# Adapter MLP kernel: a B table stored twice with one gather DMA a sequence, plain products in the first step, and the sums of h stored from the sync queue

## The chip, the cores and the metric

One core of one Trainium2 chip. The metric is the device time of one execution in microseconds; lower is better. Engines are named as the profile names them: PE (TensorE), DVE (VectorE), ACT (ScalarE), POOL (GpSimd), SP (SyncE, which here only issues DMAs).

## The reference

64 sequences of 64 tokens, width 512, each with an adapter number 0 to 7 (`itok_B_0_7`, known only when the kernel runs).

```
def lora_linear(x, W, A, B, a):             # A: (8, in, 16), B: (8, 16, out)
    return x @ W + (x @ A[a]) @ B[a]
gate, up = lora_linear(x, Wg, Ag, Bg, a), lora_linear(x, Wu, Au, Bu, a)   # 512 -> 2048
h = silu(gate) * up
x = x + lora_linear(h, Wd, Ad, Bd, a)       # 2048 -> 512
x = x + einsum('bct,bcd->bdt', x, W1[a])    # a 64x64 matrix a sequence
```

## The kernel before

Everything is float32 from split operands: each operand is cut into a rounded part (`hi`, made by ACT, type fp32r) and the rest (`lo`, made by DVE as source minus hi), and a product is three matmuls, hi*hi, hi*lo, lo*hi (`prod`, L1368 to L1370). On top of that lies one level of a Winograd form of Strassen: a 2x2 block product costs 7 products (P1 to P7) of combined blocks instead of 8 plain ones. The combined blocks of x are T1, T2, T3, NT4 (DVE, `x_add`), those of the weights S1 to S4 (DVE, `w_add`); ACT and DVE put the results together with `keep_p1`, `keep_p5`, `keep_u2`, `make_u3`, `make_c11` and so on.

Stage one (about 0 to 822 us) makes h. It goes over 4 groups of 16 sequences (1024 tokens) and, in each, over 16 chunks of 128 columns of gate and up: 64 steps. A step is 7 products of 6 matmuls of 128x512 and 4 `lora` calls of 4 matmuls of 128x256 (L1380). Stage two (from 822 us) does the down projection in 16 pairs of tiles, reading h back from DRAM (`h_dram`).

The adapter's B rows of two chunks (a "piece") for all 16 sequences of the group lie in `bq[n % 2]`, double-buffered. Each sequence takes part in two halves of the partitions (`half`), so SP issues two DMAs of 16 rows of 4 KB a sequence (`gather_b`, L276): 32 a piece, half of them in each of two steps. They can start when the buffer is free (`p4_done`) and PE needs them in the first `lora` of every second step. The table they read, `b_dram`, holds the split B; in group 0 it is made piece by piece (`load_b`, `b_hi` on ACT, `b_lo` and `store_b` on POOL). Piece 0 skips it: `gather_raw` on SP, `bq0_hi` on ACT, `bq0_lo` on POOL. The adapter's A matrices lie in SBUF (`a_all`), and POOL copies them out sequence by sequence (`gather_a`, L447) for `lora_a` (L1398), which makes x @ A for a group.

SP works through one list in program order: for each step s the weights of step s + 2 (`load_w`, L236), the stores of h of step s - 1 (`store_even`, `store_odd`, L245; these wait for DVE's h), eight sequences of the gather, and in the third step of a group the four x blocks of the next group, 2 MB (`load_x`, L241). The sums of h blocks that the Strassen form of stage two needs (HS1 to HS4, `make_s1` to `make_s4` on DVE) are stored by POOL (`store_sum`, L473), which waits for each. DVE waits for such stores before it writes a sum's tile again.

`step_0` is written out by hand on every engine. On PE it holds the 7 products with the `lora_a` calls between them, and it waits for T1 to NT4 and S1 to S4 of the first step.

## Time and profile before

| | us |
|---|---|
| median of 3 runs | 1217.3 (1215.41 to 1223.75) |
| the profiled execution | 1219.65 |
| its span, first to last instruction | 1218.0 |
| PE, DVE, ACT, POOL busy | 1163.6, 913.6, 539.3, 256.3 |
| mean granted TensorE clock | 0.982 |

Busy times are sums over the span. A granted clock of 1.00 is 2.4 GHz and one of 0.50 is 1.2 GHz.

### The profile page before, as it was taken

What the parts mean: (1) busy time and instruction counts of PE and PEld (TensorE: products, weight loads), DVE (VectorE), ACT (ScalarE), POOL (GpSimd) and SP (SyncE); (2) the same over time, 40 slices, a digit from 0 to 9 for tenths busy, and PEclk for the clock granted to TensorE, in tenths of its full rate; (3) what the DMA queues carried; (4) which work ended last, traced back from release to release, by engine and by line L of the source; (5) the groups of instructions that cost most, each with busy time, mean ns of one, the idle gap of its engine ahead of it and who ended that gap; (6) DMA issues with size and microseconds to landing.
All of it is one profiled execution on the core that took longest, in us unless ns stands there. A gap on an engine that the chain in (4) does not pass through costs nothing.

```text
span 1218.0 us, 23035 instructions
## 1 busy us (share of the span) xinstructions
PE 1163.6 (96%) x6720; PEld 1034.8 (85%) x6720; DVE 913.6 (75%) x1578; ACT 539.3 (44%) x902; POOL 256.3 (21%) x405
## 2 busy tenths in 40 slices
PE   4889999999999997999999999998899999999998
PEld 3678888887888886888888788887899999999997
DVE  6776777876787787678887788888667766776775
ACT  4544444543444443344453344456344444444442
POOL 5223221112201012220101111011322221231230
PEclk8899999999999999899999999999999999999999
DMA  5597876688667589666759978868777777667781
GB/s 188 161 308 241 244 222 180 170 235 262 189 180 234 171 238 264 190 194 187 233 166 274 280 223 252 243 215 307 244 265 244 244 239 273 232 230 274 231 277 66
DMA packets 155583, 276.26 MB, mean 227 GB/s; under 512 B 28898, under 2 KB 97634, under 8 KB 155330
## 3 DMA queue, kind: packets, MB, share of 16 engines
q1 hardware_dynamic: 133104, 213.48, 57.5%
q0 software_dynamic: 21488, 59.66, 14.6%
q10 hardware_dynamic: 866, 1.66, 0.4%
q8 instruction: 54, 0.88, 0.3%
q14 instruction: 71, 0.58, 0.2%
HBM read 200.23 MB, written 74.45 MB: 226 GB/s over the span
## 4 chain that ended last, share of the span: by engine, by line
PE 73%; SPq 9%; DVE 5%; DMA 5%; issue 4%; ACT 3%; POOL 1%; POOLq 0%; DVEq 0%; ACTq 0%
PE ps L1368 12%; PE ps L1369 12%; PE ps L1370 12%; PE ps L1517 8%; PE ps L1519 8%; PE ps L1518 8%; PE ps L1380 7%; SPq L276 7%; DMA bq<-b_dram 2%; PE ps L1398 2%; DMA h_raw<-h_dram 1%; DMA xst<-xg 1%; SPq L245 1%; ACT xo_hi L602 1%; SPq L199 1%
## 5 line engine op out<-in xcount | busy, mean ns | idle before, releaser
L1368 PE MATMUL ps<-xo_hi,w_hi 128*128 128x512 f32 x896 | 359.3, 401 | 12.0 <-DVE w_lo L886 10.7
L1369 PE MATMUL ps<-xo_lo,w_hi 128*128 128x512 f32 x896 | 354.8, 396 | 0.0
L1370 PE MATMUL ps<-xo_hi,w_lo 128*128 128x512 f32 x896 | 351.8, 393 | 0.0
L1368 PEld LDWEIGHTS ps<-xo_hi,w_hi 128*128 128x128 f32 x896 | 171.4, 191 | 43.0 <-DVE w_lo L886 10.7
L1370 PEld LDWEIGHTS ps<-xo_hi,w_lo 128*128 128x128 f32 x896 | 170.4, 190 | 38.2
L473 POOL DMA_DIRECT2D h_dram<-hs x128 | 96.0, 754 | 487.3 <-DVE hs L1001 247.9
L886 DVE TENSOR_TENSOR hl<-h_raw,hh 128x1024 fp32r<-128x1024 f32 x112 | 137.0, 1223 | 79.0 <-ACT hh L602 77.6
L1380 PEld LDWEIGHTS ps<-t_st,bq 128*128 128x128 f32 x1024 | 158.5, 193 | 44.2 <-DMA bq<-b_dram 18.0
L1369 PEld LDWEIGHTS ps<-xo_lo,w_hi 128*128 128x128 f32 x896 | 171.1, 191 | 26.6
L1380 PE MATMUL ps<-t_st,bq 128*128 128x256 f32 x1024 | 166.2, 286 | 21.7 <-DMA bq<-b_dram 15.9
L602 ACT ACTIVATE hh<-h_raw 128x1024 fp32r<-128x1024 f32 x112 | 117.9, 1053 | 113.3 <-DMA h_raw<-h_dram 72.0
L886 DVE TENSOR_TENSOR w_lo<-wsum,w_hi 128x512 fp32r<-128x512 f32 x116 | 83.1, 717 | 60.2 <-ACT w_hi L602 60.2
L674 ACT ACTIVATE u_s<-u_s 128x512 f32<-128x512 f32 x64 | 40.5, 633 | 145.6 <-DVE u_s L973 145.6
L1517 PE MATMUL ps<-wd_t,hh 128*128 128x256 f32 x256 | 73.2, 286 | 5.5 <-DVE hl L886 3.8
L1517 PE MATMUL ps<-wd,hh 128*128 128x288 f32 x256 | 76.6, 299 | 0.0
L986 DVE TENSOR_TENSOR h_f<-u_s,v 128x512 f32<-128x512 f32 x64 | 44.2, 690 | 41.7 <-ACT u_s L674 41.7
L1518 PE MATMUL ps<-wd,hh 128*128 128x288 f32 x256 | 75.4, 295 | 0.0
L670 ACT ACTIVATE p_s<-p_s 128x512 f32<-128x512 f32 x64 | 40.5, 633 | 78.5 <-DVE p_s L956 78.4
L1519 PE MATMUL ps<-wd,hl 128*128 128x288 f32 x256 | 75.2, 294 | 0.0
L602 ACT ACTIVATE w_hi<-wsum 128x512 fp32r<-128x512 f32 x116 | 72.2, 623 | 5.4 <-DVE wsum L919 5.4
L1518 PE MATMUL ps<-wd_t,hh 128*128 128x256 f32 x256 | 72.9, 285 | 0.0
L1519 PE MATMUL ps<-wd_t,hl 128*128 128x256 f32 x256 | 72.9, 285 | 0.0
(153 smaller groups left out, 2188.0 us busy)
## 6 DMA issues: line engine op xcount, KB each, us to landing
bq<-b_dram SPq DMA_DIRECT2D x992, 64.0 KB, 2.6
h_raw<-h_dram SPq DMA_DIRECT2D x112, 512.0 KB, 5.3
h_dram<-hs POOLq DMA_DIRECT2D x128, 256.0 KB, 4.2
raw<-packed SPq DMA_DIRECT2D x58, 512.0 KB, 4.0
...
xs<-x POOLq DMA_DIRECT2D x16, 512.0 KB, 5.8
...
```

Source lines behind the costliest of these rows:

```text
L276: sp.dma_start(bq[n % 2][r:r + RANK, b // QS, :, :].bitcast(F32).rearrange("r k c -> r (k c)"), b_dram[piece_of(g, k), bass.ds(slot_number ...
L473: pool.dma_start(h_dram[PPG * g:PPG * (g + 1), op, :, k, :].rearrange("q p t -> p q t"), tile[:, col:col + HALF].rearrange("p (q t) -> p q ...
L602: return act.activation(dst, src, ACT.Copy)
L886: return dve.tensor_tensor(dst, src, hi.bitcast(F32), ALU.subtract)
L986: dve.tensor_tensor(h_f[s % 2][:, HALF:GT], u2_s[:, :], v22[:, :], ALU.mult).then_inc(h2_done, 1)
L1368: pe.matmul(bank, st[0], mv[0], start=start and kk == 0, stop=False, skip_group_check=True)
L1369: pe.matmul(bank, st[0], mv[1], start=False, stop=False, skip_group_check=True)
L1370: m = pe.matmul(bank, st[1], mv[0], start=False, stop=kk == 1, skip_group_check=True)
L1380: m = pe.matmul(bank[:, i * QT:(i + 1) * QT], b[:, q, c % PIECE, a:a + P], t_st[u][g % 2][:, q * QT:(q + 1) * QT], start=start and part == ...
L1517: pe.matmul(bank[:, 0:width], h_hi, w[:, 0:width], start=start and k == 0, stop=False, skip_group_check=True)
L1518: pe.matmul(bank[:, 0:width], h_hi, w[:, width:2 * width], start=False, stop=False, skip_group_check=True)
L1519: return pe.matmul(bank[:, 0:width], h_lo, w[:, 0:width], start=False, stop=False, skip_group_check=True)
```

## The change

- **B table.** `b_dram` gets a dimension of two copies; `store_b` writes each piece twice (two DMAs). A sequence's 32 rows (two halves of 16) are then one block, fetched by one DMA of 32 rows of 4 KB into every fourth partition (`b % QS:P:QS`). 16 gathers a piece instead of 32. For piece 0 the host gives `b_twice`, a doubled input, and `gather_raw` issues 16 DMAs instead of 32. `slot_mask` and the A operand change their order of rows to match.
- **A.** `a_all` and its 512 KB load go. POOL fetches a sequence's A (128 rows of 512 B, 64 KB) by a DMA each, from DRAM, four a quad, 16 a group; ACT (first group) or POOL (`order_a`, one 512-column copy a quad) puts it in order.
- **First step.** PE does 8 plain products (48 matmuls instead of 42) of the blocks B11, B12, B21, B22 and the raw weights, which need no T or S. T1 to NT4 are made later, for step 1; S1 to S4 of step 0 are not made. The results need no `keep_p1`, `keep_p5`, `keep_u2`, `make_u3` in step 0. The first product of step 1 (`first_product`) is put ahead of the last two `lora` calls of step 0. T3 and `bq0_lo` go from POOL to DVE.
- **Stores of the sums.** `store_s12`, `store_s3`, `store_s4` go from POOL to SP, behind the gathers of the same step; the last ones (`n == 8`, `n == 11` of stage two) too. POOL's list in a step is then `order_a`, `gather_a`, tables, and `b_lo`, `store_b`, `load_b`.
- The waits that counted the removed operations are counted anew (`w_added`, `p1_kept`, `u3_done` one less).

In the diff below, left out are the renamed semaphores, the counts of waits, the row orders and the helpers that only cut a known operation into parts (`w_hi_first`, `w_lo_first`: columns 0 to 255, 256 to 767, 768 to 1023 of the weights).

```
-        b_dram = nc.dram_tensor("b_dram", (PIECES, ADAPTERS, RANK, PIECE * BC), F32, kind="Internal").ap()
+        b_dram = nc.dram_tensor("b_dram", (PIECES, ADAPTERS, 2, RANK, PIECE * BC), F32, kind="Internal").ap()
...
             def load_w(s):
                 n = load_no(s)
-                if n >= 2:
+                if n == 2:
+                    sp.wait_ge(w_lo_done, 3)
+                if n >= 3:
                     sp.wait_ge(w_lo_done, 3 * (n - 2) + 1)
-                    sp.wait_ge(w_added, 4 * (n - 1))
+                    sp.wait_ge(w_added, 4 * (n - 2))
                 sp.dma_start(raw[s % 2][:, :], packed[chunk_of(s)]).then_inc(w_in[s % 2], 16)
 
...
+            def store_s3(n):
+                sp.wait_ge(hs3_done, n + 1)
+                store_op(2 * n, HS3, hs3, 0)
+
+            def store_s12(n):
+                sp.wait_ge(hs1_done, n + 1)
+                store_op(2 * n, HS1, hs1, 0)
+                sp.wait_ge(hs2_done, n + 1)
+                store_op(2 * n, HS2, hs2, 0)
+
+            def store_s4(n):
+                sp.wait_ge(hs4_done, n + 1)
+                store_op(2 * n, HS4, hs2, 0)
+
...
                 slot_numbers[b] = number(sp, b)
-                for half in range(2):
-                    r = half * QR + (b % QS) * RANK
-                    sp.dma_start(bq_raw[r:r + RANK, b // QS, :, :],
-                                 b_gu[0, bass.ds(slot_numbers[b], 1)].rearrange("a r k c -> (a r) k c"))\
-                        .then_inc(bq_raw_in[2 * b // SLOTS], 16)
+                sp.dma_start(bq_raw[b % QS:P:QS, b // QS, :, :].rearrange("r k c -> r (k c)"),
+                             b_twice[bass.ds(slot_numbers[b], 1)].rearrange("a r c -> (a r) c"))\
+                    .then_inc(bq_raw_in[2 * b // SLOTS], 16)
 
             def gather_b(n, first, last):
                 g, k = divmod(n, PIECES)
-                sp.wait_ge(b_stored, 16 * (k if g == 0 else PIECES))
+                sp.wait_ge(b_stored, 32 * (k if g == 0 else PIECES))
                 if n >= 2:
                     sp.wait_ge(p4_done, 2 * n - 2)
                 for b in range(first, last):
-                    for half in range(2):
-                        r = half * QR + (b % QS) * RANK
-                        sp.dma_start(bq[n % 2][r:r + RANK, b // QS, :, :].bitcast(F32).rearrange("r k c -> r (k c)"),
-                                     b_dram[piece_of(g, k), bass.ds(slot_numbers[g * SLOTS + b], 1)].rearrange("a r c -> (a r) c"))\
-                            .then_inc(bq_in[n % 4], 16)
+                    sp.dma_start(bq[n % 2][b % QS:P:QS, b // QS, :, :].bitcast(F32).rearrange("r k c -> r (k c)"),
+                                 b_dram[piece_of(g, k), bass.ds(slot_numbers[g * SLOTS + b], 1)].rearrange("a e r c -> (a e r) c"))\
+                        .then_inc(bq_in[n % 4], 16)
...
                     gather_b(s // 2 + 1, at, at + SLOTS // 2)
+                if s % 2:
+                    store_s3(s // 2)
+                    if s >= 3:
+                        store_s4(s // 2 - 1)
+                else:
...
         def _(pool):
             def gather_a(g, q):
                 if g:
-                    pool.wait_ge(t_done, g * QUADS + q)
+                    pool.wait_ge(a_ordered, g * QUADS + q)
                 for s in range(QS):
                     a = number(pool, g * SLOTS + q * QS + s)
-                    pool.tensor_copy(aq[q if g == 0 else 0][:, :, s, :], a_all[:, bass.ds(a, 1), :, :].rearrange("p a k r -> p (a k) r"))\
-                        .then_inc(a_gathered, 1)
+                    pool.dma_start(a_raw[0 if g else q + 1][:, s, :, :].rearrange("p k r -> p (k r)"),
+                                   a_gu[bass.ds(a, 1)].rearrange("a p c -> (a p) c")).then_inc(a_in[q], 16)
+
+            def order_a(g, q):
+                pool.wait_ge(a_in[q], 16 * QS * (g + 1))
+                pool.wait_ge(t_done, g * QUADS + q)
+                pool.tensor_copy(aq[0][:, :, :, :], a_raw[0][:, :, :, :].rearrange("p s k r -> p k r s")).then_inc(a_ordered, 1)
...
             def store_b(i):
                 pool.wait_ge(b_lo_done, i + 1)
-                pool.dma_start(b_dram[(i + 1) % PIECES].rearrange("a r c -> (a r) c"),
-                               b_hl[:, :, :].bitcast(F32).rearrange("p k c -> p (k c)")).then_inc(b_stored, 16)
-
...
 
             load_b(0)
-            pool.wait_ge(x_in[B12], 16)
-            pool.wait_ge(x_in[B22], 16)
-            pool.tensor_tensor(xst[T3][:, :], xst[B22][:, :], xst[B12][:, :], ALU.subtract).then_inc(t3_first, 1)
+            pool.wait_ge(idx_in, 16)
+            for q in range(QUADS):
+                gather_a(0, q)
             b_lo(0)
             store_b(0)
-            pool.wait_ge(idx_in, 16)
-            pool.wait_ge(a_in, 16)
-            for q in range(QUADS):
-                gather_a(0, q)
             load_b(1)
-            for pair in range(2):
-                bq0_lo(pair)
             for s in range(1, STEPS):
                 g, c = divmod(s, CH)
                 late = LATE_T if g == 0 else 0
+                if g + 1 < GROUPS and 4 <= c - late < 8:
+                    order_a(g + 1, c - late - 4)
+                if g + 1 < GROUPS and 3 <= c - late < 7:
+                    gather_a(g + 1, c - late - 3)
+                if s == 2 * CH:
+                    load_tables()
+                if s == 2 * CH + 3:
+                    store_tables()
                 if s < PIECES:
                     b_lo(s)
                     store_b(s)
                     if s + 1 < PIECES:
                         load_b(s + 1)
-                if g + 1 < GROUPS and 4 <= c - late < 8:
-                    gather_a(g + 1, c - late - 4)
-                if s == 2 * CH:
-                    load_tables()
...
             act.dma_start(idx_i[0:1, :], idx).then_inc(idx_in, 16)
             act.dma_start(xst[B21][:, :], xg[0, :, B21]).then_inc(x_in[B21], 16)
             act.dma_start(xst[B22][:, :], xg[0, :, B22]).then_inc(x_in[B22], 16)
-            act.dma_start(a_all[:, :, :, :], a_gu).then_inc(a_in, 16)
             act.dma_start(smask[:, :], slot_mask).then_inc(const_in, 16)
             act.dma_start(tmask[:, :], tok_mask).then_inc(const_in, 16)
...
+            def order_a_first(q):
+                act.wait_ge(a_in[q], 16 * QS)
+                hi(aq[q][:, :, :, :], a_raw[q + 1][:, :, :, :].rearrange("p s k r -> p k r s")).then_inc(a_ordered, 1)
...
+            w_hi_first(0)
+            w_hi_first(1)
             x_first(B21)
+            w_hi_first(2)
+            x_hi_b12()
+            x_first(B22)
+            order_a_first(0)
             b_hi(0)
-            w_hi_sum(0, 0)
-            keep_p1(0)
+            w_hi_raw(1)
+            order_a_first(1)
             x_first(T1)
             x_first(T2)
-            w_hi_sum(0, 1)
+            bq0_hi(0)
+            order_a_first(2)
+            t_hi(0, 0)
+            w_hi_sum(1, 0)
+            t_hi(0, 1)
+            order_a_first(3)
+            t_hi(0, 2)
             x_first(T3)
-            x_first(B22)
-            t_hi(0, 0)
-            keep_p5(0)
-            x_first(NT4)
-            t_hi(0, 1)
-            keep_u2(0)
-            w_hi_raw(1)
-            t_hi(0, 2)
-            bq0_hi(0)
-            w_hi_sum(1, 0)
+            bq0_hi(1)
             t_hi(0, 3)
             w_hi_sum(1, 1)
-            bq0_hi(1)
             silu_1(0)
+            keep_p1(1)
             silu_2(0)
+            x_first(NT4)
             act.wait_ge(const_in, 48)
             hi(eye_r[:, :], eye_f[:, :])
...
+            def keep_c11_first():
+                dve.wait_ge(p2_done, 1)
+                dve.tensor_copy(p1_s[:, :], RB[0]).then_inc(c11_done, 1)
+
+            def keep_c22_first():
+                dve.wait_ge(l22_done, 1)
+                dve.tensor_copy(v22[:, :], RD).then_inc(v22_done, 1)
+
+            def keep_c12_first():
+                dve.wait_ge(p3_done, 1)
+                dve.tensor_copy(u2_s[:, :], RC[0]).then_inc(c12_done, 1)
...
@@ -1177,44 +1212,48 @@
                 x_lo(0, XOPS.index(op))
 
             x_first(B11)
-            w_lo_raw(0)
+            w_lo_first(0)
+            w_lo_first(1)
             x_first(B21)
-            for k in range(4):
-                w_add(0, k)
+            w_lo_first(2)
+            x_lo_b12()
+            x_first(B22)
             x_add(0, 1, None)
-            w_lo_sum(0, 0)
             x_add(0, 2, None)
-            x_first(T1)
-            x_first(T2)
-            w_lo_sum(0, 1)
-            dve.wait_ge(const_in, 48)
-            t_mask(0, 0)
-            x_first(T3)
-            t_lo(0, 0)
-            x_add(0, 3, None)
-            x_first(B22)
-            t_mask(0, 1)
-            x_first(NT4)
-            t_lo(0, 1)
             for k in range(4):
                 w_add(1, k)
             w_lo_raw(1)
+            x_first(T1)
+            x_first(T2)
+            bq0_lo(0)
+            dve.wait_ge(const_in, 48)
+            t_mask(0, 0)
+            t_lo(0, 0)
+            w_lo_sum(1, 0)
+            t_mask(0, 1)
+            x_add(0, 0, None)
+            t_lo(0, 1)
             t_mask(0, 2)
-            make_u3(0)
             t_lo(0, 2)
-            w_lo_sum(1, 0)
+            x_first(T3)
             t_mask(0, 3)
+            bq0_lo(1)
             t_lo(0, 3)
+            keep_c11_first()
             w_lo_sum(1, 1)
-            make_c11(0)
-            make_c22(0)
-            make_c12(0)
+            keep_c22_first()
+            make_h1(0)
+            keep_c12_first()
+            x_add(0, 3, None)
+            make_h2(0)
+            x_first(NT4)
             for s in range(1, STEPS - 1):
                 g, c = divmod(s, CH)
                 first, last = c == 0 and g > 0, c == CH - 1 and g + 1 < GROUPS
...
+            def ready(op):
+                pe.wait_ge(x_lo_done, x_turn(0, XOPS.index(op)) + 1)
+
+            def plain(bank, w, k, start, x_hi_sem, x_lo_sem, x_count, w_count):
+                wc = [slice(w * WB + kk * P, w * WB + (kk + 1) * P) for kk in range(2)]
+                xc = [slice(kk * HALF, (kk + 1) * HALF) for kk in range(2)]
+                pe.wait_ge(w_hi_done, w_count)
+                pe.wait_ge(x_hi_sem, x_count)
+                for kk in range(2):
+                    pe.matmul(bank, w_hi[0][:, wc[kk]], xo_hi[k][:, xc[kk]], start=start and kk == 0, stop=False,
+                              skip_group_check=True)
+                pe.wait_ge(x_lo_sem, x_count)
+                for kk in range(2):
+                    pe.matmul(bank, w_hi[0][:, wc[kk]], xo_lo[k][:, xc[kk]], start=False, stop=False, skip_group_check=True)
+                pe.wait_ge(w_lo_done, w_count)
+                for kk in range(2):
+                    m = pe.matmul(bank, w_lo[0][:, wc[kk]], xo_hi[k][:, xc[kk]], start=False, stop=kk == 1,
+                                  skip_group_check=True)
+                return m
+
             def step_0():
-                def ready(op):
-                    pe.wait_ge(x_lo_done, x_turn(0, XOPS.index(op)) + 1)
-
-                pe.wait_ge(w_lo_done, 1)
-                ready(B11)
-                prod(RA[0], 0, A11, 0, True).then_inc(p1_done, 1)
-                ready(B21)
-                prod(RB[0], 0, A12, 3, True)
+                a11, a12, a22, a21 = range(4)
+                plain(RB[0], a11, 0, True, x_hi_done, x_lo_done, 1, 1).then_inc(p1_done, 1)
+                plain(RB[0], a12, 3, False, x_hi_done, x_lo_done, 2, 2).then_inc(p5_done, 1)
+                plain(RA[0], a22, 3, True, x_hi_done, x_lo_done, 2, 2).then_inc(p6_done, 1)
+                plain(RA[0], a21, 0, False, x_hi_done, x_lo_done, 1, 3)
                 lora_a(0, 0)
+                plain(RC[0], a11, 6, True, b12_hi_done, b12_lo_done, 1, 1)
+                plain(RD, a21, 6, True, b12_hi_done, b12_lo_done, 1, 3).then_inc(p7_done, 1)
                 lora_a(0, 1)
-                pe.wait_ge(w_lo_done, 2)
-                ready(T1)
-                prod(RC[0], 0, S1, 1, True).then_inc(p5_done, 1)
+                plain(RC[0], a12, 5, False, x_hi_done, x_lo_done, 3, 2)
                 lora_a(0, 2)
-                pe.wait_ge(p1_kept, 1)
-                ready(T2)
-                prod(RA[0], 0, S2, 2, False).then_inc(p6_done, 1)
+                plain(RD, a22, 5, False, x_hi_done, x_lo_done, 3, 2)
                 lora_a(0, 3)
-                pe.wait_ge(u2_kept, 1)
-                pe.wait_ge(w_lo_done, 3)
-                ready(T3)
-                prod(RA[0], 0, S3, 4, False).then_inc(p7_done, 1)
-                pe.wait_ge(p5_kept, 1)
-                ready(B22)
-                prod(RC[0], 0, S4, 5, False)
-                pe.wait_ge(u3_done, 1)
-                ready(NT4)
-                prod(RA[0], 0, A22, 6, False)
                 pe.wait_ge(bq0_lo_done, 1)
                 pe.wait_ge(t_lo_done, 4)
                 lora(RB[0], 0, 0, 0, False).then_inc(p2_done, 1)
                 lora(RA[0], 0, 1, 0, False).then_inc(p4_done, 1)
+                first_product(1)
                 pe.wait_ge(bq0_lo_done, 2)
                 pe.wait_ge(t_lo_done, 2 * QUADS)
-                lora(RD, 0, 1, 1, True).then_inc(l22_done, 1)
+                lora(RD, 0, 1, 1, False).then_inc(l22_done, 1)
                 lora(RC[0], 0, 0, 1, False).then_inc(p3_done, 1)
+
+            def first_product(s):
+                g, c = divmod(s, CH)
+                pe.wait_ge(w_lo_done, 3 * load_no(s) + 1)
+                if c == 0:
+                    pe.wait_ge(x_lo_done, 7 * g + 1)
+                if s == 1:
+                    pe.wait_ge(t_masked, 2)
+                if s >= 2:
+                    pe.wait_ge(h1_done, s - 1)
+                prod(RA[s % 2], s, A11, 0, True).then_inc(p1_done, 1)
```

## Rows read from the trace of the kernel before

**Rows 1.** Busy time by stretch: us, PE, PEld, DVE, ACT, POOL busy, clock, DMA share, GB/s.

```profile
225.00:425.00 200.00, 198.00 (x992) 167.70 (x991) 155.22 (x257) 89.68 (x144) 32.29 (x48) 1.00 0.71 208
```

**Rows 2.** Who PE waited for: us in total, times, longest us.

```profile
PE ps L1380 <- DMA bq<-b_dram: 15.9, 5, 7.2
PE ps L1380 <- POOL bq L468: 5.9, 2, 3.7
PE ps L1398 <- POOL aq L447: 4.9, 1, 4.9
```

**Rows 3.** Timeline of PE, first matmuls of steps 0 and 2: start, us.

```profile
10.73 0.79 PE L1368 MATMUL ps<-xo_hi,w_hi 128*128 128x512 f32 x1 [10.73 <-DVE w_lo L886]
60.13 0.40 PE L1368 MATMUL ps<-xo_hi,w_hi 128*128 128x512 f32 x1
60.36 0.40 PE L1369 MATMUL ps<-xo_lo,w_hi 128*128 128x512 f32 x1
```

**Rows 4.** The profile's chain that ended last, by line.

```profile
PE ps L1368 12%; PE ps L1369 12%; PE ps L1370 12%; PE ps L1517 8%; PE ps L1519 8%; PE ps L1518 8%; PE ps L1380 7%; SPq L276 7%; DMA bq<-b_dram 2%; PE ps L1398 2%; DMA h_raw<-h_dram 1%; DMA xst<-xg 1%; SPq L245 1%; ACT xo_hi L602 1%; SPq L199 1%
```

**Rows 5.** Timeline of PE after two waits for gathers.

```profile
90.94 1.22 PE L1380 MATMUL ps<-t_st,bq 128*128 128x256 f32 x4 [4.20 <-DMA bq<-b_dram]
...
94.44 0.40 PE L1368 MATMUL ps<-xo_hi,w_hi 128*128 128x512 f32 x1
...
487.62 1.22 PE L1380 MATMUL ps<-t_st,bq 128*128 128x256 f32 x4 [7.16 <-DMA bq<-b_dram]
...
493.74 0.63 PE L1380 MATMUL ps<-t_st,bq 128*128 128x256 f32 x4
```

**Rows 6.** SP's queue around two group starts, then issue times (min/median/max ns).

```profile
270.40 1.84 SPq L241 DMA_DIRECT2D xst<-xg  x4
273.77 8.50 SPq L276 DMA_DIRECT2D bq<-b_dram  x16
...
456.35 12.94 SPq L276 DMA_DIRECT2D bq<-b_dram  x16
...
L276 SPq DMA_DIRECT2D bq<-b_dram x992: 315/367/3064, 29.3 to 797.5; - x199
L245 SPq DMA_DIRECT2D h_dram<-h_f x96: 371/388/1592, 50.4 to 832.1; - x96
```

**Rows 7.** Two stretches of the busy-time view: x blocks, then gathers and stores.

```profile
78.00:81.00 3.00, 3.00 (x17) 2.51 (x16) 3.00 (x4) 0.09 (x1) 2.53 (x4) 1.00 1.02 404
...
480.00:487.60 7.60, 0.46 (x3) 0.04 (x1) 4.29 (x8) 2.33 (x4) 1.50 (x2) 0.73 1.06 253
```

**Rows 8.** DMA queues: packets, MB, share of 16 engines; and one group of issues.

```profile
q1 hardware_dynamic: 133104, 213.48, 57.5%
q0 software_dynamic: 21488, 59.66, 14.6%
...
b_dram<-b_hl POOLq DMA_DIRECT2D x8, 512.0 KB, 3.4
```

**Rows 9.** Timeline of ACT and DVE in the first step.

```profile
7.49 1.06 ACT L602 ACTIVATE xo_hi<-xst 128x1024 fp32r<-128x1024 f32 x1 [1.45 <-DMA xst<-xg]
...
8.58 1.22 DVE L886 TENSOR_TENSOR xo_lo<-xst,xo_hi 128x1024 fp32r<-128x1024 f32 x1 [8.58 <-ACT xo_hi L602]
...
32.52 0.42 DVE L914 TENSOR_TENSOR wsum<-raw 128x256 f32<-128x256 f32 x1
```

**Rows 10.** Timeline of PE at the start of stage two.

```profile
827.80 0.40 PE L1517 MATMUL ps<-wd_t1a,hh 128*128 128x288 f32 x1 [2.20 <-DVE hl L886]
```

**Rows 11.** Paced lists of SP (first gather; load_ad) and POOL (gaps; a DMA).

```profile
3.73 24.88 SPq L264 DMA_DIRECT2D bq_raw<-b_gu  x32
...
802.83 3.95 SPq L357 DMA_DIRECT2D ad_raw<-a_d  x4
...
POOL mix_hi L536 <- issue: 45.5, 63, 1.4
...
L453 POOL DMA_DIRECT2D b_raw<-b_gu x8: 561/578/702, 1.4 to 121.6; - x8
```

170 lines of the change are left out of this document (87 added, 83 removed).

## The prediction

> **What bounds the kernel now.** I read the busy time by stretch first. In a stretch in the middle of stage one PE is busy 198 of 200 us, at full clock [rows 1]: there nothing but PE's own work counts, and the change leaves that work as it is. So a gain can only come from places where PE stands still, and the view of PE's waits names them [rows 2]. Two kinds matter. At the start PE does nothing until 10.73 us [rows 3], then waits 4.9 us for POOL's copies of A and 5.9 us for POOL's split of the first B piece. Later it waits five times, 15.9 us in all, for a gather of B. Only then the chain of work: it puts 7% of the span on SP issuing gathers and 2% on gathers in flight [rows 4]. The 7% is far more than PE's 15.9 us, since the chain follows slack paths through SP too; what can be won is what PE waits, with what the clock adds. I take the clock from PE's timeline behind two waits [rows 5]: matmuls run at half speed (1.2 GHz) from 90.94 to 94.44 us after a wait of 4.2 us, and from 487.62 to 493.74 us after one of 7.2 us. The other three waits, of 0.6, 1.7 and 2.2 us at 139, 288 and 685 us, repeat this, and the last has 3.4 us at half speed too.
>
> **The gathers.** Three of the five (at 87, 286 and 480 us) lie in the fifth step of a group, two steps after x for the next group is loaded. SP's queue shows why [rows 6]: x blocks 1.84 us, then sixteen gathers 8.50 us, 0.53 us each, to 282.3, and in group 2 the sixteen before x took 12.94 us. SP's load in two steps (24.4 us) is 32 gathers at 0.49 to 0.53 us, 16 us, two weight loads and three stores at about 0.5 us: 18.2 us, and 20 with x. After it: 16 gathers, 8 us, two weight loads, seven stores: 12.5 us. This needs a DMA of 32 rows to cost SP what one of 16 costs. A store of 512 rows issues in 388 ns, a gather of 16 in 367 [rows 6], so rows hardly count: I take 0.50 us, ends 0.49 and 0.98 (double). The half gathered behind x is then issued some 4 us sooner, and x itself 4 us sooner.
>
> The other side is the DMA engines. From 480 to 487.6 us they were full (share 1.06) but moved 253 GB/s, against 404 GB/s with x blocks in flight [rows 7]: gathers and stores of h use them poorly. Counting the bytes on SP's queue from the x blocks to the last gather of the piece: 2 + 0.5 + 0.25 + 1 = 3.75 MB, at 330 GB/s, midway between the two rates, 11.4 us. With x issued at 266.4 instead of 270.4 the last byte is moved at 277.8 and the gather has landed by 281; PE wants it at 286.4. In group 2 the wait of 7.2 us would shrink by the 4 to 9 us that SP is sooner. So most of the 15.9 us goes, and the half speed behind it: half of 3.5, 6.1 and 3.4 us, 6.4 us. Gone at most 22.3; I leave 3 standing, with ends 0 and 22.3.
>
> A gather fills sixteen neighbouring partitions now, and every fourth of all 128 after. The Trainium skill (SBUF — State Buffer, Door 1: the DMA port swizzle) gives four neighbouring partitions one port, so that sixteen reach 4 of 16 ports and the new pattern all 16. By that rule the gathers would move faster as well and the 3 us would be 0; the low rate in [rows 7] agrees, but stores are mixed into it.
>
> **The stores of the sums.** 128 DMAs of 256 KB in rows of 512 B move from POOL's queue to SP's. The two queues' packets can be solved for a cost: 14.6% of 16 x 1218 is 2,845 engine-us for 59.7 MB in 21,488 packets, 57.5% is 11,206 for 213.5 MB in 133,104 [rows 8], which gives 41 us a MB and 0.018 us a packet. POOL's queue packs 2.8 KB to a packet; on SP's each row would be one, 53,500 more, 976 engine-us or 61 us of all 16. Over 775 us of stage one at a share of 0.71 [rows 1] that makes 0.79, and with 7 MB more traffic (4 for the second B copies, 3 for A) 0.81. Not full on average; it lengthens the bursts, which is why I leave 3 us and not 0. SP waits for DVE's sums only behind the gathers of the step, and the next thing behind that is the weights two steps ahead: covered by about a step. In the last step of a group the sums come late, and SP stands until the next step starts, where it would wait for h in any case: nothing. At the end of stage one it is not covered: two sums of 512 columns (0.61 us each, between [rows 9]) and their issue follow the store ahead of them, 1.3 us, and behind them is the load of the NT4 weights, which PE already waits for through DVE [rows 10]. Cost 1.3 us, ends 0 and 2.5.
>
> **The first step.** PE starts when the hi parts of B11 and of a quarter of the weights are there: ACT begins at 7.49 and takes about 1 us for 1024 columns [rows 9], so at 8.8 instead of 10.73. Its work to the end of step 0 at full speed is 48 matmuls at 0.23 [rows 3], 11.0, `lora_a` four times about 1.7, `lora` four times 0.5, the first product of step 1 1.4: 21 us, and 2.5 for some 5 us at half speed ([rows 5] show 3.5 to 6.1): 32.5. DVE is later. Its list from 8.58 to the last `t_lo` is 12 operations of 1024 columns at 1.13 (1.22 less the overlap), ten of 256 at 0.34 (0.42 less the same) [rows 9], between these two of 512 (0.61) and one of 768 (0.87), four pairs of `t_lo` (0.87): 22.6 us, and 2.5 of waits for ACT's `t_hi` between mask and `t_lo`: 33.7. PE's last two `lora` calls wait for that. From there DVE does c11, a weight sum, c22, h1, c12 (3.0), `x_add` and NT4 (2.3), h2 (0.6), weights and sums of step 2 (4.1), c11 and u3 of step 1 (1.3), 0.6 of waits: 45.6. PE's last product of step 1 needs that u3; its own work would bring it there at 44.3. Then 1.9 us: step 2 starts at 47.5. Before it started at 60.13 [rows 3]. Gain 12.6 us.
>
> What else must be in time. POOL fetches A one sequence after another: POOL's gaps are 0.72 us each (45.5 / 63), with 0.58 for the DMA 1.3 us [rows 11], sixteen 20.8 us; with 3.4 us to land [rows 8] the quads are there from 3.7 us on at 12.3, 17.5, 22.7 and 27.9. PE wants them at 17.6, 22, 25 and 28: covered, the last one barely. SP's first gather took 24.88 us for 32 [rows 11]; with 16, at 1.0 to 1.1 us with the number's load (3.95 us for four), it ends at 21 and PE wants it at 30. The next gather waits for POOL's store behind A's fetches, is issued by 42, and PE wants it at 50. In later groups POOL's one ordering copy a step stands for four and is wanted a step later: nothing. If PE finds only POOL late here, about 8 of the 12.6 us go.
>
> **Sum.** 1219.65 - 12.6 - 22.3 + 3 + 1.3 = 1189.1 for the profiled execution, which lay 2.35 over the median: 1187.
>
> **The rivals** (all less 2.35).
> - Bandwidth keeps the waits: the engines are full in these stretches whoever issues [rows 7], so an earlier issue lands no earlier. 1219.65 - 12.6 + 1.3 is 1206. Against it: 3.75 MB fit. 0.15.
> - The first step pays only 4 us, because A's fetches or the long DVE list slip: 1196. 0.13.
> - The second B copies hold group 0 back. One store lands in 3.4 us now [rows 8]; if each landed in twice that, the gather of the third piece would start 3.5 us late with x behind it, and one wait like the first (4.2 + 1.7) stays: 1193. 0.10. The Trainium skill (DMA: Bandwidth & Descriptors, Why a DMA increments its semaphore by 16 and not by 1) says that the number of DMA engines is the largest divisor up to 16 common to the outermost dims; the new store's DRAM side starts with 8 adapters, which gives 8 engines.
> - It does not relieve SP: a gather of 32 rows costs 0.98 us. Then SP has 15.7 + 4.5 = 20.2 us of work in two steps instead of 18.2, the five waits grow by 2 us each: 1216. 0.05.
> - Slower: sums in 512 B packets fill the engines around every load of x. The place is the three group starts and the wd loads in group 3, the price a wait of 10 us (7.2 and 3 of clock, the worst now) at each, and 3 us in each of seven steps of group 0, where B copies add most: 61 us. 1219.65 - 12.6 - 22.3 + 61 is 1243. It decides against the change from waits of 57 us in all, up from 22. 0.05.
>
> **How the numbers follow.** The forecast has 0.52: 1187. The range takes the ends of its terms: all waits gone and the first step 3 us better, 1180, a little below for faster gathers, 1176; at the upper side the bandwidth rival at 1206: 1207. Outside are the last two rivals. A measurement tells 1% here, about 12 us. Faster: 0.52 + 0.13 + 0.10 and 0.09 of the bandwidth case, which sits on the bound: 0.84. Same: its other 0.06 and the 0.05 of SP: 0.11. Slower 0.05.
>
> **What would show it.** Right: PE's first matmul before 9.5 us and step 2 at 46 to 50; no wait for POOL in step 0; waits for gathers under 5 us in all; SP's gathers in eights of 4 us; a mean share of the DMA engines over 0.75 in stage one. Wrong: a gather issue near 1 us; waits for gathers still at the fifth step of each group; PE waiting for A in step 0; a longer wait than 2.2 us at the first down product. The number fails most easily by the first step, where DVE has no slack from 9 to 46 us and each wait inside is passed on to PE.

## The result and the profile after

The changed kernel takes 1224.3 us (median; 1223.5 to 1226.8), the kernel before 1217.1: a ratio of 1.0074, with a 95% interval of 1.0044 to 1.0105. The forecast was 1187, with a range of 1176 to 1207. The profiled execution has a span of 1225.1 us, against 1218.0.

To see where the time went, read PE's timeline at five places: the start of the last `lora` call of step 1 (it ends the first step's part), and the start of the last `lora` call in the last step of each group. The distances from one place to the next, us:

| | to step 1 | group 0 | group 1 | group 2 | group 3 | rest | span |
|---|---|---|---|---|---|---|---|
| before | 59.7 | 177.2 | 194.1 | 202.3 | 188.5 | 396.2 | 1218.0 |
| after | 49.9 | 202.7 | 192.1 | 197.5 | 184.5 | 398.4 | 1225.1 |

The first step gives 9.8 us and groups 1 to 3 give 10.8. Group 0 takes 25.5, more than both together, and the rest 2.2.

Who PE waited for, as in [rows 2]:

```profile
PE ps L1407 <- DVE v L998: 14.1, 6, 5.9
PE ps L1419 <- DMA bq<-b_dram: 11.7, 3, 4.5
PE ps L1450 <- ACT w_hi L594: 8.6, 1, 8.6
PE ps L1407 <- ACT p_s L658: 3.7, 1, 3.7
PE ps L1419 <- DVE t_st L896: 1.9, 1, 1.9
```

POOL is gone from the list, and gathers went from 15.9 us to 11.7. New is DVE's `v`, for which PE waited 1.1 us before. Where these waits lie is in PE's timeline:

```profile
8.64 1.22 PE L1450 MATMUL ps<-xo_hi,w_hi 128*128 128x512 f32 x2 [8.64 <-ACT w_hi L594]
...
50.38 0.40 PE L1407 MATMUL ps<-xo_hi,w_hi 128*128 128x512 f32 x1
...
77.64 0.80 PE L1407 MATMUL ps<-xo_hi,w_hi 128*128 128x512 f32 x1 [5.90 <-DVE v L998]
88.93 1.22 PE L1419 MATMUL ps<-t_st,bq 128*128 128x256 f32 x4 [4.46 <-DMA bq<-b_dram]
...
130.03 0.80 PE L1407 MATMUL ps<-xo_hi,w_hi 128*128 128x512 f32 x1 [3.68 <-ACT p_s L658]
146.54 1.03 PE L1419 MATMUL ps<-t_st,bq 128*128 128x256 f32 x4 [3.72 <-DMA bq<-b_dram]
160.55 0.79 PE L1407 MATMUL ps<-xo_hi,w_hi 128*128 128x512 f32 x1 [5.27 <-DVE v L998]
```

PE starts at 8.64 us and reaches step 2 at 50.38, where it was at 60.13 before [rows 3]. All waits of over 3 us in stage one but one (3.5 us for a gather at 497 us) lie before 165 us, which is the time in which the B table is made and stored. What else is in that stretch is told by the view of DMA issues (KB each, median us from issue to landing), for the changed kernel:

```profile
bq<-b_dram SPq DMA_DIRECT2D x496, 128.0 KB, 2.6
b_dram<-b_hl POOLq DMA_DIRECT2D x16, 512.0 KB, 9.2
b_raw<-b_gu POOLq DMA_DIRECT2D x8, 256.0 KB, 11.0
```

A gather of 32 rows lands as fast as one of 16 did. But a store of a B piece takes 9.2 us, where it took 3.4 [rows 8], and the load of the next piece, issued behind two of them on POOL's queue, takes 11.0 (5.4 before). SP, ACT and DVE stand for that, one by one. First SP. POOL's and SP's timelines:

```profile
46.32 1.23 POOL L492 DMA_DIRECT2D b_dram<-b_hl  x2 [0.30 <-POOL b_hl L486]
47.54 0.59 POOL L482 DMA_DIRECT2D b_raw<-b_gu  x1
60.04 1.29 POOL L486 TENSOR_TENSOR b_hl<-b_raw,b_hl 128x512 fp32r<-128x512 f32 x1 [11.91 <-ACT b_hl L594]
```

```profile
51.23 3.33 SPq L249 DMA_DIRECT2D h_dram<-h_f  x2
58.14 9.61 SPq L290 DMA_DIRECT2D bq<-b_dram  x8
67.81 2.08 SPq L249 DMA_DIRECT2D h_dram<-hs  x2
69.93 2.83 SPq L245 DMA_DIRECT2D xst<-xg  x4
74.39 9.38 SPq L290 DMA_DIRECT2D bq<-b_dram  x8
```

The same gather in the kernel before:

```profile
61.86 7.79 SPq L276 DMA_DIRECT2D bq<-b_dram  x16
```

There it starts 1.7 us after PE's step 2 does. Here the stores issued at 46.32 let SP start it only at 58.14, 7.8 us after step 2, and the stores of the sums, x and the second half of the gather follow. ACT, which works in order, stood at its split of B in group 0 (waits by releaser, 0 to 245 us; the kernel before has no such line; then the longest of these waits in ACT's timeline):

```profile
ACT b_hl L594 <- DMA b_raw<-b_gu: 30.1, 5, 8.8
```

```profile
126.13 0.63 ACT L594 ACTIVATE b_hl<-b_raw 128x512 fp32r<-128x512 f32 x1 [8.78 <-DMA b_raw<-b_gu]
```

Behind that split DVE waits 6.0 us for ACT's `u_s`, and PE 3.7 us for ACT's `p_s` at 130.03 (`u_s`, `p_s` and `v` are results on the way to h). DVE itself stood for the stores of the sums, which had not landed when it wanted to write the next sum:

```profile
74.50 0.69 DVE L1054 TENSOR_TENSOR hs<-h_f,hs 128x512 f32<-128x512 f32 x1 [8.45 <-DMA h_dram<-hs]
...
76.91 0.68 DVE L998 TENSOR_TENSOR v<-ps,p_s 128x512 f32<-128x512 f32 x1
...
156.80 0.69 DVE L1048 TENSOR_TENSOR hs<-hs,h_f 128x512 f32<-128x512 f32 x1 [8.40 <-DMA h_dram<-hs]
```

SP had issued the first of these stores at 67.81, behind the late gather, and the second at 144.46, behind another. `v` comes behind the sum in DVE's list, and so these two waits are PE's of 5.90 and 5.27 us. PE was busy 179.3 of the 202.7 us of group 0, where it was busy 171.7 of 177.2 before: 17.9 of the 25.5 us are more standing, and 7.6 are the same work at a lower clock, granted at 0.95 in this stretch and at 0.99 before.

In the middle of stage one nothing of this is left. Busy time by stretch, as in [rows 1], and the queues, as in [rows 8]:

```profile
225.00:425.00 200.00, 199.71 (x1001) 169.30 (x1000) 161.00 (x266) 89.15 (x144) 7.78 (x11) 1.00 0.71 214
```

```profile
q1 hardware_dynamic: 192496, 247.01, 64.2%
q0 software_dynamic: 16496, 34.50, 9.6%
```

PE is busy 199.7 of 200 us; the DMA share stands at 0.71 as before, in spite of 59,392 more packets on SP's queue over the whole run. Over all of stage one behind step 1 the share went from 0.75 to 0.77.

### The profile page after: what moved, and what is told of

Its sections match the earlier page's. It is cut to its first block, busy times and chain, and to the rows that moved or that the text cites. A ratio compares the mean times of both kernels' runs of the same rounds, so it can differ in the third digit from the quotient of the medians.

```text
span 1225.1 us, 22115 instructions
## 1 busy us (share of the span) xinstructions
PE 1166.9 (95%) x6726; PEld 1037.1 (85%) x6726; DVE 916.0 (75%) x1577; ACT 540.7 (44%) x904; POOL 169.5 (14%) x294
## 3 DMA queue, kind: packets, MB, share of 16 engines
q1 hardware_dynamic: 192496, 247.01, 64.2%
## 4 chain that ended last, share of the span: by engine, by line
PE 72%; DMA 8%; DVE 6%; SPq 6%; issue 4%; ACT 4%; POOL 0%; DVEq 0%; ACTq 0%
PE ps L1407 13%; PE ps L1408 13%; PE ps L1409 13%; PE ps L1419 8%; PE ps L1576 7%; PE ps L1578 7%; PE ps L1577 7%; SPq L290 3%; DMA h_raw<-h_dram 3%; PE ps L1437 2%; DMA b_raw<-b_gu 1%; DMA bq<-b_dram 1%; DMA h_dram<-hs 1%; DMA b_dram<-b_hl 1%; SPq L249 1%
## 5 line engine op out<-in xcount | busy, mean ns | idle before, releaser
L1407 PE MATMUL ps<-xo_hi,w_hi 128*128 128x512 f32 x882 | 354.1, 401 | 18.7 <-DVE v L998 14.1
L1408 PE MATMUL ps<-xo_lo,w_hi 128*128 128x512 f32 x882 | 349.2, 396 | 0.0
L1409 PE MATMUL ps<-xo_hi,w_lo 128*128 128x512 f32 x882 | 346.5, 393 | 0.0
L1407 PEld LDWEIGHTS ps<-xo_hi,w_hi 128*128 128x128 f32 x882 | 168.4, 191 | 50.2 <-DVE v L998 16.6
L1409 PEld LDWEIGHTS ps<-xo_hi,w_lo 128*128 128x128 f32 x882 | 167.8, 190 | 37.6
L1419 PE MATMUL ps<-t_st,bq 128*128 128x256 f32 x1024 | 164.5, 284 | 13.6 <-DMA bq<-b_dram 11.7
L896 DVE TENSOR_TENSOR w_lo<-wsum,w_hi 128x512 fp32r<-128x512 f32 x114 | 79.2, 698 | 38.9 <-ACT w_hi L594 38.9
L594 ACT ACTIVATE w_hi<-raw 128x768 fp32r<-128x768 f32 (+2 forms) x60 | 49.5, 827 | 33.3 <-PE ps L1419 27.2
```

The source lines that it names most:

```text
L594: return act.activation(dst, src, ACT.Copy)
L896: return dve.tensor_tensor(dst, src, hi.bitcast(F32), ALU.subtract)
L1407: pe.matmul(bank, st[0], mv[0], start=start and kk == 0, stop=False, skip_group_check=True)
L1408: pe.matmul(bank, st[0], mv[1], start=False, stop=False, skip_group_check=True)
L1409: m = pe.matmul(bank, st[1], mv[0], start=False, stop=kk == 1, skip_group_check=True)
L1419: m = pe.matmul(bank[:, i * QT:(i + 1) * QT], b[:, q, c % PIECE, a:a + P], t_st[u][g % 2][:, q * QT:(q + 1) * QT], start=start and part == ...
```

## The experiments

The table gives all kernels by the same five places; "ratio" is to the kernel before on the same chip, with its interval. Each is told below.

| kernel | median | ratio | to step 1 | g0 | g1 | g2 | g3 | rest |
|---|---|---|---|---|---|---|---|---|
| b_store16 | 1199.0 | 0.986 (0.981 to 0.991) | 48.9 | 172.7 | 192.2 | 197.7 | 184.5 | 400.9 |
| sums_pool | 1229.8 | 1.011 (1.006 to 1.016) | 49.8 | 203.7 | 192.1 | 195.9 | 184.5 | 400.5 |
| b_two_tiles | 1207.6 | 0.992 (0.989 to 0.995) | 53.8 | 179.1 | 192.1 | 198.6 | 184.5 | 401.0 |
| b_two_tiles_pool | 1213.4 | 0.998 (0.996 to 1.001) | 52.2 | 188.9 | 192.0 | 193.3 | 184.5 | 398.5 |
| first_contig | 1209.3 | 0.994 (0.993 to 0.996) | 51.0 | 179.5 | 193.7 | 200.6 | 185.1 | 399.8 |
| before_sums_sp | 1242.8 | 1.023 (1.020 to 1.027) | 59.0 | 178.2 | 202.1 | 204.7 | 194.0 | 404.5 |
| before_store8 | 1233.1 | 1.017 (1.010 to 1.024) | 58.9 | 193.3 | 193.0 | 200.8 | 187.0 | 398.2 |
| b_interleaved | 1221.8 | 1.005 (1.002 to 1.007) | 54.3 | 183.9 | 195.6 | 200.2 | 184.5 | 398.0 |
| after_load_first | 1224.4 | 1.006 (1.004 to 1.008) | 50.1 | 200.8 | 192.1 | 197.6 | 184.5 | 399.9 |
| b_two_tiles_load_first | 1207.4 | 0.992 (0.989 to 0.995) | 52.5 | 179.0 | 192.1 | 194.7 | 184.5 | 400.6 |

Beside these, b_single took 1374.9 (1.129; 1.123 to 1.135), both_undone 1309.1 (1.075; 1.070 to 1.080) and b_copies_outer 1996.3 (1.644; 1.634 to 1.654).

**b_store16: the stores of B in another shape.** Each store goes to 128 neighbouring rows, so the rows lie at wrong places.

```
-  pool.dma_start(b_dram[(i + 1) % PIECES, :, copy],
+  pool.dma_start(b_dram[(i + 1) % PIECES].rearrange("a e r c -> (a e r) c")[copy * P:(copy + 1) * P],
```

> The changed kernel, but each of the two stores of a B piece goes to 128 neighbouring rows of the table (outermost dim 128 instead of 8 adapters). The bytes and the number of DMAs are the same. It leaves out the right place of the rows: a gather then fetches rows of other adapters. Theory E (a store whose DRAM side begins with 8 runs on fewer engines, lands late, and holds up the load of B behind it on POOL's queue, ACT, and SP's gathers): landing falls from 9.2 us to 3.4 to 5, the 25 us that group 0 lost between step 2 and step 16 mostly return, time about 1201 (1196 to 1207). Rival T (4 MB more traffic in group 0 are enough): landing stays over 7 us, time over 1219. Rival S (the stores of the sums on SP hold things up): time over 1218 too.

It took 1199.0: with the same bytes, DMAs and semaphore waits, 25 us come back, and group 0 is at 172.7, below the kernel before. Theory E's time holds; T and S fall. The stores land in 6.2 us (3.4 to 5 expected), two behind each other, the load in 7.0, and ACT's wait for it falls from 30.1 to 8.6. DVE's waits for stores of the sums fall from 22.4 us to 6.3 (40 to 250 us). The DMA queues from 40 to 170 us show what the shape does; first the changed kernel, then this one:

```profile
DMA packets 24536, 32.77 MB, mean 252 GB/s; under 512 B 4012, under 2 KB 18348, under 8 KB 24527
q1 hardware_dynamic: 19983, 23.22, 57.6%
q0 software_dynamic: 4544, 9.45, 31.2%
...
h_dram<-hs SPq DMA_DIRECT2D x15, 256.0 KB, 4.6
h_dram<-h_f SPq DMA_DIRECT2D x13, 256.0 KB, 8.7
xst<-xg SPq DMA_DIRECT2D x4, 512.0 KB, 6.4
```

```profile
DMA packets 28802, 38.84 MB, mean 299 GB/s; under 512 B 2771, under 2 KB 21715, under 8 KB 28788
q1 hardware_dynamic: 25780, 28.72, 69.9%
q0 software_dynamic: 3008, 9.96, 21.3%
...
h_dram<-hs SPq DMA_DIRECT2D x21, 256.0 KB, 4.3
h_dram<-h_f SPq DMA_DIRECT2D x16, 256.0 KB, 6.7
xst<-xg SPq DMA_DIRECT2D x4, 512.0 KB, 10.3
```

POOL's queue takes 31.2% of the engines' time for 9.45 MB, and 21.3% for 9.96 MB: 69 engine-us a MB against 44 (0.312 x 16 x 130 / 9.45, and the same for the other). Stores of h on SP's queue, which the edit leaves alone, land 2 us sooner; the x blocks land 3.9 us later, so not every other transfer gained. Over the whole run POOL's queue has 2,048 packets fewer than in the changed kernel, 128 a store, nearly all under 512 B.

**sums_pool: the sums' stores back on POOL's queue**, as in the kernel before.

> The changed kernel with the stores of the sums of h back on POOL, as before the change; the rest stays. Theory E: the late stores of B remain, so ACT still waits for B's load; only DVE's waits for stored sums (25 us in six waits, about half of it on PE's path) go: 1212 to 1218. Rival S: nearly all of group 0's loss returns: under 1204. Rival T: 1219 or more. If the packets of 512 B on SP's queue cost, groups 1 to 3 get faster as well.

It took 1229.8, 5.5 more than the changed kernel, and group 0 is as slow as before the edit. So it is not having the stores of the sums on SP that costs: rival S falls, and theory E missed by 12 us. Theory E had expected DVE's waits for these stores to go. They grow, from 22.4 us to 34.0 (40 to 250 us), and the stores now stand on POOL's queue beside B's slow ones. Rival T's number fits, but b_store16 has the same traffic and is quick.

**b_single and both_undone: one table, 16 gathered rows, every fourth partition.** Both take two DMAs of 16 rows a sequence from a table stored once; b_single leaves the sums on SP, both_undone puts them back on POOL.

```
-  sp.dma_start(bq[n % 2][b % QS:P:QS, ...], b_dram[piece, a].rearrange("a e r c -> (a e r) c"))
+  for half in range(2):
+      r = half * QR + b % QS
+      sp.dma_start(bq[n % 2][r:(half + 1) * QR:QS, ...], b_dram[piece, a].rearrange("a r c -> (a r) c"))
```

> The changed kernel with one copy of the B table, stored as 128 neighbouring rows, and two gathers of 16 rows a sequence; gather_raw, the first step, A and the sums on SP stay. Theory E: group 0's loss returns, but SP now issues 32 gathers and the sums, so the 11 us won in groups 1 to 3 are lost and the waits there grow: 1208 to 1216. Rival S: SP is fuller still: over 1220. Rival T: like E.

> The changed first step and the A fetches alone: one copy of B with two gathers of 16 rows, sums stored by POOL. All theories: step 2 starts near 50.4 us against 60.1 in the kernel before, and nothing else changes: 1207 (1204 to 1211). If the A fetches or the order of POOL's list cost something in groups 0 to 2, it is over 1211.

They missed their ranges by 159 and 98 us, and for a reason that was not in the comparison. Issue times of a gather (min/median/max ns), in the changed kernel and in both_undone; those of the kernel before, 367, are in [rows 6]:

```profile
L290 SPq DMA_DIRECT2D bq<-b_dram x496: 472/472/4005, 33.3 to 799.5; - x166
```

```profile
L278 SPq DMA_DIRECT2D bq<-b_dram x992: 495/535/3107, 27.2 to 886.3; - x199
```

Sixteen rows into every fourth partition cost SP 535 ns, sixteen into neighbouring ones 367, and 32 into every fourth 472. Sixteen such DMAs take SP about 10.7 us, so 32 a piece with the stores leave it nothing of PE's 24.4 us. These two kernels tell of SP's issue, not of the part that was undone; first_contig below takes their place.

**b_two_tiles: quick stores with every row in its place.** B is loaded twice over into two tiles of four adapters, so that a store of a tile is 128 neighbouring rows.

```
-  for copy in range(2):
-      pool.dma_start(b_dram[piece, :, copy], b_hl[:, :, :]...)
+  for t in range(2):
+      pool.dma_start(b_dram[piece, t * 4:t * 4 + 4].rearrange("a e r c -> (a e r) c"), b_hl[:, t, :, :]...)
```

> The changed kernel, but the B piece lies in SBUF in two tiles of four adapters, each with both copies in its 128 partitions, so each of the two stores writes 128 neighbouring rows and the doubled table is exact. B is loaded doubled (512 KB a piece instead of 256), and ACT's and POOL's splits of a piece take 1024 columns instead of 512. Theory E (the store in eight runs of 16 rows is what cost group 0 its 25 us): the 1199 of the run with neighbouring rows, plus a little for the longer split beside DVE: 1199 to 1206, with a B store landing in about 6 us. Theory P (the gain of that run came from the wrong placement of the rows, not from the shape of the store): 1215 to 1225. Theory D (the doubled load and split bring the lateness back): b_raw lands near 9 us and the time is 1210 or more.

At 1207.6 it is 0.992 of the kernel before; with b_two_tiles_load_first it is the best of the kernels whose table is whole, and better than both kernels compared (first_contig, at 0.994, is too near to be told from it). The stores land in 4.9 us. It is between what E and D expected, and its profile 12.2 us behind that of b_store16: the first step is 4.9 us longer and group 0 6.4. There POOL's split of a piece takes 2.4 us instead of 1.3 and the load of 512 KB lands in 8.1, for which ACT stands 24.9 us. ACT stands nearly as long as in the changed kernel, then, but DVE doesn't wait for stores of the sums at all in group 0, and group 0 is 23.6 us better: ACT's standing alone is the smaller part of the harm. Theory P falls, E's mechanism holds (its range is missed by 1.6 us), and D has a part.

**b_two_tiles_pool**: the same with the sums on POOL.

> The same with the stores of the sums back on POOL's queue. With the slow B stores in place this move cost nothing (1230 on POOL, 1224 on SP). Theory S (the sums' 512 B packets on SP's queue cost DMA time, which is hidden in the other runs): 1190 to 1198. Theory N (they cost SP an issue it can spare, and POOL's queue holds late B traffic back when it carries them): 1202 to 1212.

1213.4: theory N missed by 1.4 us. The sums on POOL's queue cost group 0 9.8 us, beside B's traffic on the same queue (DVE waits 14.7 us for them, where it waited none), and group 2 is 5.3 shorter.

**first_contig: the first step alone**, with the kernel before's B rows, gathers and sums.

> The plain products of the first step and A fetched by DMA alone, with the kernel before's rows of B (16 neighbouring partitions, two gathers a sequence, one table) and the sums on POOL. Theory F (the first step gives the 9.7 us that the trace shows at step 2 and the rest is as before): 1207 to 1209, and the five waits for gathers, some 16 us, are back. Theory G (A's fetches of 3 MB more, or the first step's early end, themselves hold group 0 back): 1213 or more, with markers of group 0 late against the kernel before.

1209.3, a little over theory F's 1207 to 1209. Against the kernel before, the profile has 8.7 us less to step 1; groups 0 to 3 differ by +2.3, -0.4, -1.7 and -3.4. PE still waits for gathers five times, 12.5 us in all. Theory G falls.

**before_sums_sp: the sums alone**, in the kernel before.

> The kernel before with one part of the change alone: the sums stored by SP behind its gathers. Theory N (the sums are harmless on SP): 1215 to 1220. Theory S (SP already has 20 of 24.4 us to do in the two steps with a gather, four more stores of about 0.4 us each and their longer packets make its gathers later): the five waits for gathers grow by 1 to 2 us each and the time is 1222 to 1230.

1242.8, worse than both theories. PE waits for gathers ten times, 22.8 us, and for `v` 7.5:

```profile
PE ps L1377 <- DMA bq<-b_dram: 22.8, 10, 5.3
...
PE ps L1365 <- DVE v L960: 7.5, 8, 2.7
```

So the stores of the sums do cost SP, when it also has 32 gathers a piece to issue; with 16 they cost nothing. The two parts of the change belong together, and the doubled table does relieve SP, as the prediction said.

**before_store8: one slow store alone.** The kernel before, with an empty second copy behind each adapter, so that its one store a piece has eight runs of 16 rows.

```
-  pool.dma_start(b_dram[piece].rearrange("a r c -> (a r) c"), b_hl...)
+  pool.dma_start(b_dram[piece, :, 0], b_hl...)          # b_dram: (PIECES, 8, 2, 16, ...)
```

> The kernel before with one edit: its B table is laid out with an empty second copy behind each adapter, so that its one store a piece writes eight runs of 16 rows; all reads are as before. Theory E: the store lands in 6.2 to 6.8 us instead of 3.4, and group 0, where the waits for gathers are few, loses 0 to 6 us: 1216 to 1222. Theory Q (one such store is as quick as a plain one, and the 9.2 us of the changed kernel come from two stores and a load standing in one queue): it lands in 3.4 to 4 us and the time is 1215 to 1218.

1233.1, 16 us more than the kernel before (ratio 1.017), all of it in group 0. The store lands in 7.7 us, not 3.4, with the queue, the count of DMAs and the bytes as they were. Only the step between adapters differs, and with it the packets: POOL's queue has 1,024 more, 128 a store again, all under 512 B. No run tells these small packets from the eight runs. PE waits for gathers for 24.7 us, 9.7 at most. Theory E had the store too quick (6.2 to 6.8) and its cost far too low; Q falls.

**b_copies_outer: the two copies one behind the other.** Now the stores have 128 neighbouring rows, and a gather reads two runs of 16.

```
-  b_dram[piece, a].rearrange("a e r c -> (a e r) c")
+  b_dram[piece, :, a].rearrange("e a r c -> e (a r) c")   # b_dram: (PIECES, 2, 8, 16, ...)
```

> The changed kernel with the two copies of the B table one after the other in DRAM: each store writes 128 neighbouring rows, and a gather reads two runs of sixteen rows, so its outermost dimension is 2 in DRAM and 32 in SBUF. Theory E (the engines are the largest common divisor up to 16 of the outermost dimensions) gives the stores 16 engines and the gathers 2: 128 KB a gather at 25 GB/s an engine (404 GB/s over 16) is 2.6 us for each of 496 one behind the other on the same two, 42 us a piece where PE has 24.4: 1500 us or more. Theory R (the rows are dealt out one by one, whatever the outermost dimension): gathers as before, fast stores, 1199 to 1206.

1996.3. Page of the profile, busy time and the issues:

```profile
h_dram<-hs SPq DMA_DIRECT2D x128, 256.0 KB, 16.1
b_dram<-b_hl POOLq DMA_DIRECT2D x16, 512.0 KB, 5.7
```

```profile
225.00:425.00 200.00, 124.48 (x518) 102.40 (x518) 93.68 (x149) 50.07 (x80) 16.23 (x24) 0.79 0.32 103
```

PE waits 411 us for gathers and 263 for `v`; DVE waits 731 us for stores of the sums, which land in 16.1. The DMA engines are busy 32% of the stretch from 225 to 425 us at 103 GB/s: transfers are waited for while most engines are idle. Gathers that crowd onto a few engines would look like that, and rows dealt out one by one over all of them would not: theory R falls. SP's queue has 6,944 packets fewer than in the changed kernel (185,552 against 192,496), 14 for each of 496 gathers, which fits a closing packet from each of 2 engines in place of 16. The Trainium skill (DMA: Bandwidth & Descriptors, Why a DMA increments its semaphore by 16 and not by 1) has the rule for the number of engines: the largest divisor up to 16 common to the outermost dimensions, 2 and 32 here, 8 and 128 for the slow stores. The landing times and this run agree with it; the trace shows no single engine's load, so that the slow stores ran on eight is argued and not seen.

**b_interleaved: sixteen runs of 8 rows.** The copies alternate by half an adapter, so that a store's outermost dimension is 16; t is split in 32-partition parts to fit.

```
+  b_dram: (PIECES, 2 * ADAPTERS, 2, RANK // 2, PIECE * BC)     # store: [:, copy], sixteen runs of 8 rows
```

> The changed kernel with the exact doubled table, one load of 256 KB and one split of 512 columns a piece, but the two copies interleaved in DRAM by eight rows (adapter, half of the rank, copy, eight rows), so that each store writes sixteen equal runs of 8 rows instead of eight of 16. A's columns are ordered to fit, and the split of t takes four parts of 32 partitions a quad instead of two of 64: 8 more short operations of ACT and of DVE a group, about 2.7 us of DVE in the first step. Theory E (what matters is how many DMA engines the outermost dimension of a store lets it use: 8 before this edit, 16 after it): a store of B lands in 6 to 7 us and the time is 1199 to 1206. Theory R (what matters is that the rows of a store aren't neighbours in DRAM): a store still takes about 9 us, and the time is 1220 to 1228.

The stores land in 6.6 us, as theory E says and R does not: their rows still aren't neighbours. The small packets are gone as well (POOL's queue has 14,448, as in b_store16). But the kernel takes 1221.8, 16 us over theory E's range, so that this run shows what a store costs by its shape and not what the kernel gains by it. Group 0 is 18.8 better than in the changed kernel; the first step is 4.4 worse. The split of t in four parts costs more than was allowed for. ACT takes 1.7 us a quad for it instead of 0.85, and in the first step PE waits 4.4 us for the `aq` behind it, 1.8 in the changed kernel. DVE's row for it, in this kernel and in the changed one:

```profile
L899 DVE TENSOR_TENSOR t_st<-t_f,t_st 32x256 fp32r<-32x256 f32 x64 | 26.7, 417 | 5.1 <-ACT t_st L594 4.0
```

```profile
L896 DVE TENSOR_TENSOR t_st<-t_f,t_st 64x256 fp32r<-64x256 f32 x32 | 13.4, 420 | 1.9 <-ACT t_st L594 1.0
```

PE waits 18 times for `v`, 18.9 us in all, mostly under 1 us each. Groups 1 and 2 take 3.5 and 2.7 us more than in the changed kernel. Its profiled execution (1218.2 us) is the quickest of its ten, so the median is nearer to the changed kernel's than the rows are.

**after_load_first and b_two_tiles_load_first: which way the slow store hurts.** POOL issues the load of the next piece ahead of the stores.

```
-  store_b(s); load_b(s + 1)
+  load_b(s + 1); store_b(s)
```

> The changed kernel with one exchange: POOL issues the load of the next B piece ahead of the two slow stores of this one, not behind them. In the changed kernel ACT stood 30.1 us in group 0 at its split of B waiting for these loads, which it did for 8.6 us with quick stores and never in the kernel before. Theory A (the slow stores do their harm through the load queued behind them and ACT, which stands in order and keeps the chunk's products waiting): the load lands in 3 to 6 us, ACT's wait for it is under 8 us, and 10 to 20 of the 25 us of group 0 come back: 1204 to 1214. Theory L (the harm is the late landing of the stores themselves, for which SP's gathers and ACT's next split wait whatever the load does): 1218 to 1228.

> The same exchange in the version with the table in two tiles, whose ACT stood 24.9 us for loads of B. Theory A: 4 to 8 us better than the 1207.6 of that version, 1199 to 1204. Theory L: no change, 1205 to 1210.

1224.4 and 1207.4: no change in either. The load lands in 4.3 us instead of 11.0, yet ACT stands all the same, now for the stores, since `b_hi` may overwrite `b_hl` only when they have landed:

```profile
ACT b_hl L594 <- DMA b_dram<-b_hl: 17.1, 4, 6.7
```

Theory A falls. ACT stands less in all (17.1 us against 30.1), but DVE's waits for stores of the sums are 25.9 us, where they were 22.4 (40 to 250 us), and PE waits 9.4 us for gathers and 11.8 for `v` (50 to 250 us). The stores' own late landing holds SP's gather and what SP issues behind it, and ACT; the load behind them was one more that came late, not the way the harm took.

## Why the prediction was wrong

**The step that failed is the price of the second B copies.** The sum put it at nothing, and the rival at 1193, with a chance of 0.10, at 6 us. The rival had the place right, the late landing of the new store, and named eight engines for it; its size was wrong. It took twice 3.4 us and counted one late gather, with one wait of 6 us left standing. A store lands in 9.2 us, 2.7 times as long, and every piece of group 0 has two: 30 us, the difference between the changed kernel and b_store16 (202.7 less 172.7). The step was read as the delay of one consumer. The traces show three: SP's gather, ACT's next split, and DVE, which stood for the sums' stores that SP had issued behind the late gather. Of PE's long waits in group 0, 11.2 us lead to DVE's standing, 8.2 to gathers and 3.7 to ACT's; no run takes one of the three away alone. With 30 us in the sum for it the forecast would have been 1217, and the two terms below, mis-sized by some 3 and 4 us, make most of the rest. The range's upper end, 1207, came from the bandwidth rival and had no room for this.

**The first step** was forecast at 12.6 and gave 9.8 (8.7 in first_contig, 10.8 in b_store16). PE began at 8.64 (forecast 8.8). DVE was late, as the text feared: POOL's split of B lies beside DVE's split of `bq0`, and DVE's timeline shows what that costs:

```profile
21.95 2.29 DVE L896 TENSOR_TENSOR bq<-bq_raw,bq 128x1024 fp32r<-128x1024 f32 x1
...
33.22 1.21 DVE L896 TENSOR_TENSOR bq<-bq_raw,bq 128x1024 fp32r<-128x1024 f32 x1
```

The same operation takes 1.21 us alone. Beside the first one is POOL's split:

```profile
21.77 1.39 POOL L486 TENSOR_TENSOR b_hl<-b_raw,b_hl 128x512 fp32r<-128x512 f32 x1
```

PE also waited 1.8 us for `aq`, 1.9 for `t_st` and, in step 1, 2.3 for `v`.

**The gathers' waits.** Forecast: 22.3 gone (half of 3.5, 6.1 and 3.4 is 6.5 and not 6.4, so 22.4), less 3 left standing, 19.3. With the stores quick (b_store16 against the kernel before) groups 0 to 3 give 4.5, 1.9, 4.6 and 4.0, 15.0 in all, and one wait of 3.7 us is left at 467 us. The mechanism held, and the term was 4 too large. The issue of 32 rows was taken at 0.50; the instruction is 472 ns, but in groups 1 to 3 eight take 5.1 to 6.3 us, 0.7 each with the address, where sixteen mostly took 7.5 to 9 before, so SP is relieved by 5 to 6 us a piece and not by 8.

**The sums.** At the end of stage one +1.3 was forecast. The rest of the span is 398 to 401 in all kernels with the change, and 398.2 in before_store8, whose code there is the kernel before's; so no more than a few tenths of the 2.2 us are shown to be the change's. As much stands in PE's wait for `xs` in stage two, 3.9 us against 1.7, and before_store8 has 4.0. The wait in which the 1.3 us would show hardly moved from the 2.20 of [rows 10]:

```profile
832.80 0.56 PE L1576 MATMUL ps<-wd_t1a,hh 128*128 128x288 f32 x1 [2.28 <-DVE hl L896]
```

The slower rival (512 B packets fill the engines) fell: the DMA share stayed at 0.71 in the middle of stage one, where the sum had put 0.79 for the packets alone, and it is 0.77 over stage one, where it had put 0.81. The SP rival (0.98 us an issue) fell as well.

**The port rule** (SBUF — State Buffer, Door 1: the DMA port swizzle, in the Trainium skill) gives quicker gathers. A gather of 32 rows landed in 2.6 us, as one of 16 did, so a byte of it was quicker, but with the number of rows changed as well no run tells the ports apart.

The account closes: 9.8 (first step) + 10.8 (groups 1 to 3) - 25.5 (group 0) - 2.2 (rest) = -7.1, the two spans' difference.
